# A four-layer residual kernel: where TensorE's loop turns back, and three edits to the setup

## The reference, cut to what matters

```python
# x: 64 sequences x 64 tokens x 512, float32
x = x + L0(x)   # x @ W.T, plus an adapter of rank 16 picked per sequence, scaled
x = x + L1(x)   # tokens mixed in each sequence by one of 200 tables of 64x64
x = x + L2(x)   # causal attention, 16 heads of 32, q scaled by min(cond, 4)/sqrt(32)
x = x + L3(x)   # tokens mixed in each sequence by one of 8 tables of 64x64
```

## Time and profile before

| what | us |
|---|---|
| three runs: median (lowest to highest) | 613.75 (613.18 to 613.85) |
| the profiled execution: its own time | 613.62 |
| its span, first to last instruction | 611.9 |
| TensorE busy | 603.4 (99% of the span) |
| weight loads / DVE / ACT / POOL busy | 521.6 / 392.5 / 224.5 / 109.9 |
| mean granted TensorE clock | 0.997 |

### The profile page before, as it was taken

One profiled execution on the slowest core, in us unless ns is written; L12 is line 12 of the kernel. 1 busy time (PEld: TensorE's weight loads), 2 busy tenths in 40 slices (PEclk: granted clock), 3 DMA queues, 4 the chain that ended last, 5 costly groups with the idle time before them and its releaser, 6 DMA issues.

```text
span 611.9 us, 21509 instructions
## 1 busy us (share of the span) xinstructions
PE 603.4 (99%) x8534; PEld 521.6 (85%) x8534; DVE 392.5 (64%) x573; ACT 224.5 (37%) x434; POOL 109.9 (18%) x101
## 2 busy tenths in 40 slices
PE   9999999899999999999999999999999999999998
PEld 8798889788898988889788898988889898888885
DVE  4789865665657666575765657567575766647374
ACT  4545451342514334152442424344251443513222
POOL 2004030301303021040401204030030302103030
PEclk9999999899999999999999999999999999999999
DMA  9862323222222323223222322322222231210312
GB/s 297 163 135 58 84 61 77 75 61 74 63 72 77 92 65 71 73 58 79 73 64 73 79 73 65 88 73 60 74 63 73 74 82 54 66 70 4 71 41 104
DMA packets 65272, 48.29 MB, mean 79 GB/s; under 512 B 16922, under 2 KB 51738, under 8 KB 65242
## 3 DMA queue, kind: packets, MB, share of 16 engines
q1 hardware_dynamic: 60090, 42.63, 26.8%
q10 hardware_dynamic: 5152, 5.24, 3.0%
HBM read 30.54 MB, written 17.30 MB: 78 GB/s over the span
## 4 chain that ended last, share of the span: by engine, by line
PE 96%; DVE 2%; issue 1%; ACT 0%; DVEq 0%
PE banks L654 10%; PE banks L649 10%; PE banks L650 10%; PE banks L677 5%; PE banks L748 5%; PE banks L679 5%; PE banks L749 5%; PE banks L755 5%; PE banks L681 5%; PE banks L589 5%; PE banks L591 5%; PE banks L593 5%; PE banks L702 5%; PE banks L694 4%; PE banks L718 3%; PE banks L633 3%
## 5 line engine op out<-in xcount | busy, mean ns | idle before, releaser
L649 PE MATMUL banks<-x1T_hi,w_hi 128*128 128x256 f32 x512 | 129.8, 286 | 0.0
L650 PE MATMUL banks<-x1T_hi,w_lo 128*128 128x256 f32 x512 | 128.2, 283 | 0.0
L649 PEld LDWEIGHTS banks<-x1T_hi,w_hi 128*128 128x128 f32 x512 | 98.0, 191 | 0.5 <-ACT x1T_hi L914 0.2
L650 PEld LDWEIGHTS banks<-x1T_hi,w_lo 128*128 128x128 f32 x512 | 98.1, 192 | 0.0
L654 PE MATMUL banks<-x1T_lo,w_hi 128*128 128x256 f32 x512 | 82.4, 283 | 0.1
L1429 POOL TENSOR_TENSOR probs<-probs,row_max 128x1024 f32<-128x1024 f32 x32 | 61.0, 1905 | 115.4 <-DVE row_max L1209 115.4
L1411 POOL TENSOR_TENSOR w_own<-w_in,own 128x128 f32<-128x128 f32 x32 | 14.9, 466 | 362.5 <-PE banks L616 267.5
L654 PEld LDWEIGHTS banks<-x1T_lo,w_hi 128*128 128x128 f32 x512 | 70.6, 192 | 0.4 <-DVE x1T_lo L1120 0.3
L1195 DVE TENSOR_TENSOR qkT<-banks,beta 128x512 f32<-128x512 f32 x32 | 22.0, 689 | 60.4 <-PE banks L654 60.4
L914 ACT ACTIVATE x_y<-banks 128x512 f32<-128x512 f32 (+1 forms) x17 | 9.9, 585 | 128.8 <-PE banks L616 122.0
L1213 DVE TENSOR_REDUCE row_sum<-probs 128x16 f32<-128x1024 f32 x32 | 39.0, 1218 | 25.1 <-ACT probs L996 25.1
(11 more groups left out here) (138 smaller groups left out, 1057.3 us busy)
## 6 DMA issues: line engine op xcount, KB each, us to landing
x_rows<-x_in SPq DMA_DIRECT2D x64, 128.0 KB, 2.4
x_kept<-x_rows SPq DMA_DIRECT2D x16, 512.0 KB, 3.6
x_in<-in_x_dram SPq DMA_DIRECT2D x60, 128.0 KB, 2.8
out_dram<-x_y SPq DMA_DIRECT2D x15, 512.0 KB, 3.0
b_sel<-b_parts SPq DMA_DIRECT2D x180, 32.0 KB, 1.7
w_in<-in_L_cond_weights_dram SPq DMA_DIRECT2D x128, 16.0 KB
probsT<-in_L_cond_W_dram ACTq DMA_DIRECT2D x1, 1024.0 KB, 6.3
probs<-in_L_cond_Wk_dram ACTq DMA_DIRECT2D x1, 1024.0 KB, 6.0
```

The lines of the kernel that those rows point to most:

```text
L649: nc.tensor.matmul(out_ap, w_hi[:, w, c, cols], x1T_hi[:, c, :], start=(c == 0), stop=False)
L650: nc.tensor.matmul(out_ap, w_lo[:, w, c, cols], x1T_hi[:, c, :], start=False, stop=False)
```

## The change

In TensorE's loop the scores move from the end of a step to its beginning: pass i now computes `scores(i)` and then `values(i, ·)`, and the last thing ahead of the turn is `attend(i)`. The waits for the copies of y move into `scores`, and since they now also stand ahead of `scores` in step 1 and later by the same formula, SP raises both semaphores by one at its start, and all other waits for them count one higher. In step 13, the first behind the loop, the order is `values(13, 0)`, `scores(13)`, `values(13, 1)`; steps 14 and 15 have the scores first. In the setup the second `stay_busy` issues 3 products instead of 8, Bm is turned behind layer 0's first chunk instead of ahead of it, and DVE turns WV's part 0 together with the three others.

```diff
         def _(sp):
+            sp.sem_inc(y_copied_act, 1)
+            sp.sem_inc(y_copied_dve, 1)
             sp.sem_inc(y_stored, 1)
...
             def store_y(i):
-                sp.wait_ge(y_copied_act, i + 1)
-                sp.wait_ge(y_copied_dve, i + 1)
+                sp.wait_ge(y_copied_act, i + 2)
+                sp.wait_ge(y_copied_dve, i + 2)
...
             def scores(i):
+                if after(i, -1):
+                    pe.wait_ge(y_copied_act, i)
+                    pe.wait_ge(y_copied_dve, i)
...
             def step(i):
                 prev, nxt, nxt2 = after(i, -1), after(i, 1), after(i, 2)
                 if not prev:
+                    scores(i)
                     pe.wait_ge(part_split, len(PARTS_V))
-                values(i, 0)
-                if prev:
+                    values(i, 0)
+                elif parted(i) and i == LAST_ALIKE + 1:
+                    pe.wait_ge(q_scaled, 2 * i + 1)
+                    values(i, 0)
+                    scores(i)
                     values(i, 1)
+                else:
+                    scores(i)
+                    for t in range(TILES):
+                        values(i, t)
...
-                if prev:
-                    pe.wait_ge(y_copied_act, i)
-                    pe.wait_ge(y_copied_dve, i)
-                else:
+                if not prev:
                     pe.wait_ge(part_split, len(PARTS_V) + len(PARTS_O))
-                scores(i + 1)
...
-            stay_busy(8)
+            stay_busy(3)
...
-            pe.wait_ge(b_ordered, 1)
-            turn(GROUP_B, [b_nat[:, c, :] for c in range(NC)], in_rows_of_b)
             for c in range(NC):
                 pe.wait_ge(turned_lo, GROUPS_OF[W0][c] + 1)
                 for t in range(TILES):
                     layer0_part(t, c)
                 if c == 0:
+                    pe.wait_ge(b_ordered, 1)
+                    turn(GROUP_B, [b_nat[:, n, :] for n in range(NC)], in_rows_of_b)
                     first_adapters_down()
...
             adapters_down(1)
-            scores(0)
             in_steps(pe, step)
...
             first_x1_copy()
-            turn_w(0)
             for c in (1, 2):
                 take_lo(GROUPS_OF[WQ][c], w_lo[:, WQ, c, :], w_hi[:, WQ, c, :])
...
-            for n in PARTS_V[1:]:
+            for n in PARTS_V:
                 turn_w(n)
```

More of the change, by code:

```diff
@@ L495, in _ @@
             for t in range(TILES):
-                sp.wait_ge(y_copied_act, PAIRS + t)
+                sp.wait_ge(y_copied_act, PAIRS + 1 + t)
                 if t == 1:
-                    sp.wait_ge(y_copied_dve, PAIRS)
+                    sp.wait_ge(y_copied_dve, PAIRS + 1)
                 sp.dma_start(out_v[PAIRS - 1][:, t, :], y[:, t, :]).then_inc(y_stored, 16)
@@ L903, in _ @@
             pe.wait_ge(x2_added, TILES * PAIRS)
-            pe.wait_ge(y_copied_act, PAIRS - 1)
+            pe.wait_ge(y_copied_act, PAIRS)
             for n, to in enumerate((MIX[1], OUT[0])):
```

## The result

The changed kernel takes 614.9 us (median of 19 runs, 614.7 to 615.4), the one before beside it 613.85 (19 runs, 612.36 to 614.9): the ratio is 1.0021, interval 1.0014 to 1.0028. It is slower by 1.3 us by that ratio, where no change that can be measured was forecast. The time lies inside the range, yet not where the forecast put it. The profiled execution took 614.97 us, 1.35 more than that of before.

| stretch | before | after | difference | forecast |
|---|---|---|---|---|
| start to `scores(0)` | 40.20 | 39.05 | −1.15 | −1.5 |
| start to `attend(1)` | 105.95 | 104.75 | −1.20 | −1.5 |
| `attend(1)` to `attend(2)` | 39.98 | 36.84 | −3.14 | −3.31 |
| `attend(2)` to `attend(12)`, ten passes | 363.96 | 367.56 | +3.60 | +2.9 |
| `attend(12)` to `attend(13)` | 33.37 | 35.46 | +2.09 | +1.7 |

The account below looks back on a forecast made before the run. TensorE (PE), on the critical chain for 96% of the time, was taken to bound the kernel. The terms −3.6 − 1.8 + 5.0 + 1.7 − 1.5 = −0.2 us turned 613.62 into 613.4 us, range 610.6 to 615.8.

Parts of the forecast that it names:

- Part 1: End of the loop's first pass: the scores' 1.6 us gap and the clock's fall behind it go, −3.6 us.
- Part 2: Between scores and values: the loop's turn leaves this place, saving 0.16 us at each of eleven turns, −1.8 us.
- Part 3: Between attend and scores: the turn in its new place costs 0.45 us, times 11, +5.0 us.
- The bound of 0.66: Turn between attend and scores: upper cost per turn if waits at the loop's head come on top, +7.3 us in all.
- The rival of a cheap turn: Turn between attend and scores: costs only 0.16 us there too, +1.8 in all, time 610.2 us; chance 0.21.
- Part 4: Step 13: values(13, 0) ahead of scores(13) delays the softmax by 2.7 us and so layer 1, +1.7 us.
- Part 5: Setup: fewer products of zeros, Bm's transposes later and WV's first part turned later, together −1.5 us.
- (b): Setup: Bm's transposes go behind layer 0's first chunk, removing waits for a bank and for a_all, −0.3 us.
- (c): Setup: turn_w(0) leaves the chain PE waits for 0.51 us at 27.09, so the keys begin at 27.3, −0.6 us.
- The clock did not fall at the turns: Rival: silence at the loop's turns lowers the clock, 1.7 us each; two falls give 616.8 us; chance 0.08.
- The wait for code did not move to the loop's end or to the first turn: Rival: step 13's scores or the first turn wait for code instead, price 3.6 us, time 617.0 us; chance 0.06.
- the turns fetched nothing: Rival: each of eleven turns forces an instruction fetch, a wait like the 1.60 us one, 631 us; chance 0.02.

Follow-up runs that it names:

- The two last runs: The changed kernel without the scores' two waits for copied keys, 613.91 us; the changed kernel with three already-met waits more at the scores' head, 618.67 us.
- The run in the common order: The changed kernel with step 13 computing scores(13) first, then both values, instead of its special order: 613.44 us, ratio 0.9990.
- the run with six products: The changed kernel with six of the values' 24 products ahead of the turn and the scores, step 13 like the others: 614.51 us, ratio 1.0009.

## Why the prediction was wrong

**Part 1 (first end of the loop, −3.6): right.** The stop and the fall of the clock went. The pass took 36.84, 0.17 more than forecast: 0.07 is part 3, 0.03 its turn's gap of 0.49 where the eleven have 0.46 in the mean, some hundredths stay open. That the stop is a wait for new code was inferred; the shorter setup, which moved it by nine products, the three products between, which halved it, and the packet 2.3 to 2.5 us ahead of its end in seven traces showed it.

**Part 2 (the turn leaves, −0.16 each): right**, measured 0.16.

**Part 3 (the turn in its new place, 0.45 each): the step that failed most, by its size and not by its mechanism.** It measured 0.52, so +5.7 over eleven turns and not +5.0. "0.42 and 0.03 for the one register instruction more" took a register instruction's own 0.03 us for its price. It takes a slot of 0.1, and three instructions stood behind the MOVE, 0.33 us in all; the seam before, with its waits hidden behind `attend`, was no measure of them. That `attend` hides little was right: of the sequencer's 0.75 it covered 0.23. The two last runs show that these instructions count in full. The bound of 0.66 was the place to look. The rival of a cheap turn falls.

On this branch the Trainium skill ("Advanced Engine Details and Errata", section "Control Flow Timing") gives about 108 ns; the trace has 212 at the new place too and disagrees.

**Part 4 (step 13, +1.7): right in mechanism, 0.4 too small.** The stretch grew by 2.09. DVE's copy came 2.72 later as reckoned and ended 17.6 us after `attend(12)`. But "`layer1` can't start before 527.6" put the wait behind all of L587. The last two of its products wait as well: they start at 17.77 and layer 1 at 18.08, where 17.7 was forecast. The run in the common order shows that nothing was won for this price.

**Part 5 (setup, −1.5): right in the main.** This execution shows −1.15, the run with six products, whose clock rose at 5.40 us, nearly as in that of before, −1.42. The start of the transposes at 8.32 instead of 8.1 is the clock's: in the run with the setup alone (clock at 4.00) they start at 7.91, in the one with six products at 8.05. (b) and (c) measured 0.31 and 0.46, forecast 0.3 and 0.6.

So by the table's stretches: 0.30 from the setup, 0.17 from the first pass, 0.70 from the ten passes and 0.39 from step 13 make 1.56 us; the profiled time is 614.97 − 613.4 = 1.57 over the forecast. Each is small and all point the same way. The largest share, the turn's, was within its stated bounds (0.16 to 0.66), and its upper part should have had more chance.

**The other rivals.** The clock did not fall at the turns: every gap there was under 0.8 us even with the added waits, and the granted clock stayed at 2.4 GHz. The wait for code did not move to the loop's end or to the first turn. And the turns fetched nothing: q8's 10 and 11 packets leave none for between, now with short products right behind the branch, where a fetch would have shown. The Trainium skill ("Runtime: NRT & Kernel Launch", section "Instruction fetch mechanics") has a fetch at a taken branch whose target lies outside the two pages held. In the kernel before four packets start during the loop's first pass (73.6, 86.2, 95.8 and 107.5 us) and none in a later one; so if a packet is a page, more than two were held, and the trace disagrees.

## What to carry to other kernels

In this kernel a turn took TensorE's sequencer 0.42 us and about 0.1 us more for every instruction of the waits at the loop's head, even where these are long met. What of it shows depends on the work ahead of it and behind it: 0.52 us between two blocks of short products, 0.16 from short to wide ones, nothing behind three wide ones or amid them. So count the instructions at a loop's head, and try the turn where wide work is queued before it; where extra seams would pay for that, weigh them (0.21 us here). Look also at what a first pass shows and later ones do not: where many short instructions come for the first time, a stop can be a wait for code, and three wide products between them halved it. Before work is moved ahead of a chain's start, find the first instruction that waits for the chain's end, not the block named after it; here three products fitted into the slack and six did not. The turn amid wide products together with the change's setup was not tried.

## What the runs showed of the hardware that was not expected

- The clock reached 2.4 GHz at 3.9 to 7.1 us after the start in these traces, with no edit to explain it; with the change's setup `scores(0)` then starts at 38.61 (clock at 3.94), 38.78 (5.40) and 39.06 us (7.09).
- The fall behind the stop comes in most executions and not in all: of the 30 runs of the kernel before beside the run with the turn between wide products, 26 had a mean clock of 0.997 (median 613.93 us) and 4 had 1.000 (612.93). That is the spread of the kernel before; the change, which has no such stop, spreads over 0.7 us.
- A stop of 0.76 us amid short products was followed by no fall, in the profile or in any of that kernel's seven runs; stops of 1.49 to 2.07 us mostly were. What lies between was not tried.
